# One load for the first inputs instead of two, and 13 warm-up products instead of 11, in a two-layer recurrence on one core

## What is computed

```python
# x: [32, 128 steps, 128], h0 = cond [32, 128], both layers start from it
xW = einsum('ntd,dg->ntg', x, Wx) + b
for t in range(128):
    a = xW[:, t] + h @ Wh                       # gates i, f, o, g
    c = sigmoid(f) * c + sigmoid(i) * tanh(g)   # c starts at zero
    h = sigmoid(o) * tanh(c)
x1 = x + hs
for t in range(128):
    m = concat(x1[:, t], u) @ weight + bias
    g, c = sigmoid(m[:, :128] + 1), tanh(m[:, 128:])
    u = g * u + (1 - g) * c
out = x1 + us
```

## Time and profile before

| | us |
|---|---|
| median of 3 runs (lowest to highest) | 231.49 (231.38 to 232.12) |
| the profiled execution's own time | 231.94 |
| its span, first to last instruction | 230.0 |
| PE busy | 225.1 (98%) |
| DVE busy | 200.3 (87%) |
| ACT busy | 133.8 (58%) |

### The profile page before, as it was taken

How to read it: one execution, slowest core, us unless ns; L and a number is a source line. 1 busy time by engine, 2 the same in 40 slices (tenths; PEclk the granted TensorE clock), 3 DMA queues, 4 the chain that set the end, 5 groups by cost and what they waited for, 6 DMA issues and landing times.

```text
span 230.0 us, 12260 instructions
## 1 busy us (share of the span) xinstructions
PE 225.1 (98%) x4825; PEld 212.0 (92%) x4825; DVE 200.3 (87%) x1363; ACT 133.8 (58%) x905; POOL 2.7 (1%) x11
## 2 busy tenths in 40 slices
PE   7999999999999999999999999999999999999994
PEld 6999999999999999999999999999999999999883
DVE  5457899989899999999999899999989999998995
ACT  3534665656665665666566566666656666666652
POOL 2200000000000000000000000000000000000000
PEclk9999999999999999999999999999999999999998
DMA  5100001100010000100010000100001000010001
GB/s 170 39 3 17 26 25 39 26 27 26 16 48 26 16 27 26 50 14 26 27 38 26 26 26 16 48 26 16 26 26 51 14 26 26 17 26 14 16 3 26
DMA packets 12164, 6.69 MB, mean 29 GB/s; under 512 B 1606, under 2 KB 12108, under 8 KB 12108
## 3 DMA queue, kind: packets, MB, share of 16 engines
q1 hardware_dynamic: 11952, 5.72, 8.8%
q10 hardware_dynamic: 156, 0.20, 0.2%
HBM read 3.82 MB, written 2.10 MB: 26 GB/s over the span
## 4 chain that ended last, share of the span: by engine, by line
DVE 79%; PE 9%; ACT 5%; issue 5%; DMA 1%; SPq 0%
DVE cell_bank L662 10%; DVE acts L691 10%; DVE h_low L676 10%; DVE hT L669 9%; DVE scan_add L656 7%; DVE pair L683 6%; DVE pair L685 6%; DVE h_high L670 6%; DVE u_rest L697 5%; ACT act_bank L570 5%; DVE u_low L702 3%; DVE x1T L710 3%; DVE outT L719 2%; DMA early<-in_early_dram 1%; PE a L266 1%
## 5 line engine op out<-in xcount | busy, mean ns | idle before, releaser
L282 PE MATMUL gate_f<-hT,w_f 128*128 128x32 f32 x254 | 48.8, 275 | 0.5 <-DVE hT L669 0.2
L282 PEld LDWEIGHTS gate_f<-hT,w_f 128*128 128x128 f32 x254 | 39.0, 193 | 8.5 <-DVE hT L669 8.0
L550 ACT ACTIVATE gate_f<-gate_f 128x32 f32<-128x32 f32 x127 | 23.1, 182 | 40.2 <-PE gate_f L282 40.2
L570 ACT ACTIVATE act_bank<-cell_bank 128x32 f32<-128x32 f32 x128 | 23.3, 182 | 33.4 <-DVE cell_bank L662 33.4
L662 DVE TENSOR_TENSOR_SCAN cell_bank<-act_bank,scan_add 128x64 f32<-128x64 f32 x128 | 38.2, 298 | 1.0 <-ACT act_bank L550 0.9
L576 ACT ACTIVATE acts<-a 128x64 f32<-128x64 f32 x127 | 28.3, 223 | 14.4 <-PE a L309 1.1
L300 PE MATMUL a<-h_high,w1x_scaled 128*128 128x32 f16 x254 | 35.2, 177 | 0.0
L300 PE MATMUL a<-h_high,w1x_third 128*128 128x32 f16 x254 | 35.2, 177 | 0.0
L302 PE MATMUL a<-h_low,w1x_fp 128*128 128x32 f16 x254 | 35.2, 177 | 0.0
L300 PE MATMUL a<-h_high,w1x_rest 128*128 128x32 f16 x254 | 35.1, 177 | 0.0
L669 DVE TENSOR_TENSOR hT<-out_gate,act_bank 128x32 f32<-128x32 f32 x128 | 23.9, 187 | 10.6 <-ACT act_bank L570 10.6
(11 more groups left out here) (147 smaller groups left out, 1057.3 us busy)
## 6 DMA issues: line engine op xcount, KB each, us to landing
early<-in_x_dram SPq DMA_DIRECT2D x45, 64.0 KB, 1.9
out_dram<-outT SPq DMA_DIRECT2D x31, 64.0 KB, 1.6
w_raw<-in_L_cond_weight_dram SPq DMA_DIRECT2D x2, 128.0 KB, 3.4
wh_raw<-in_L_cond_Wh_dram ACTq DMA_DIRECT2D x1, 192.0 KB, 3.0
early<-in_early_dram SPq DMA_DIRECT2D x1, 144.0 KB, 2.2
early<-in_early_dram SPq DMA_DIRECT2D x1, 128.0 KB, 2.9
w_f<-in_forget_dram SPq DMA_DIRECT2D x1, 128.0 KB, 3.4
out_dram<-outT SPq DMA_DIRECT2D x1, 48.0 KB, 1.6
```

Of the source, the lines that this page charges most:

```text
L282: nc.tensor.matmul(gate_step(GATE_F, j), w_f[:, P:2 * P], hT[:, (j - 1) % RING, :], start=False, stop=True, skip_group_check=True).then_in ...
L550: return nc.scalar.activation(out, gate_step(q, j), func)
L570: nc.scalar.activation(tanh_c[:, :], cell[:, :, 1], ACT.Tanh).then_inc(tanh_c_ready, 1)
```

## The change

Both loads from `early_in` become one, of 544 columns (272 KB), which raises `x_in[0]`. The semaphore `wx_in` and PE's wait on it are gone, so that the first projection, of gate i, waits for the whole load. The number of warm-up products ahead of that wait goes from 11 to 13. The order of PE's products, the layout of the tile and everything behind are as they were.

```diff
-WARM = 11
+WARM = 13
...
-            sp.dma_start(early[:, 2 * P:3 * P + N + HS * N], early_in[:, 2 * P:]).then_inc(x_in[0], 16)
-            sp.dma_start(early[:, 0:2 * P], early_in[:, 0:2 * P]).then_inc(wx_in, 16)
+            sp.dma_start(early[:, 0:3 * P + N + HS * N], early_in).then_inc(x_in[0], 16)
             load_x(1, 1)
...
             warm(WARM)
             pe.wait_ge(x_in[0], 16)
             project0(GATE_I, 0, 3)
-            pe.wait_ge(wx_in, 16)
             project0(GATE_O, 0, HS)
             pe.wait_ge(x_in[1], 16)
             project0(GATE_G, 0, 5)
```

More of the change, by code:

```diff
@@ L118, in two_layer_recurrence @@
         x_in = [sem(f"x_in{i}") for i in range(CHUNKS)]
-        ahead_used, wx_in = sem("ahead_used"), sem("wx_in")
+        ahead_used = sem("ahead_used")
         w_f_in, wh_in, w1x_in, w1h_in = sem("w_f_in"), sem("wh_in"), sem("w1x_in"), sem("w1h_in")
```

## The result

The changed kernel took 226.00 us (median of 4 executions: 225.66, 225.83, 226.18 and 230.91), the one before 231.48 (4 executions, 231.38 to 232.12). The ratio is 0.976, with an interval of 0.973 to 0.978. It is taken over the changed kernel's executions near 226, among them a fifth, of 226.37, that the median doesn't hold; the 230.91 is left out of it, and it is also the execution whose trace was kept. It is no stray. Both kernels turn out to have two groups of times with almost nothing between them: an early group near 226 and a late one near 231.5. Over all sets of this study the changed kernel was in the early group in 17 of 22 executions, the one before in 31 of 86 (4 more lay between, at 229.8 to 230.3).

What follows compares the result with a forecast made beforehand. PE was taken to bound 4.15 to 22.5 us, then ACT and DVE. 231.94 - 4.3 - 1.3 + 0.0 = 226.3 for the profiled execution, 225.9 for the median, given as 226.0; range 225.3 to 232.2.

Steps and rivals of the forecast that it cites:

- an early rise of the clock: PE's clock rises between 3.7 and 5 us instead of about 20.4, giving 226.0 us; chance 0.41.
- The load: The merged first load, issued at 0.73 us, lands at 3.7, with bounds of 3.29 and 4.13.
- Gate i's projection and the slip: Gate i's projection, now behind the whole load, delays gate o by 0.4 us; gate g's start slips 0.0, -0.25 to +0.45.
- The warm-up: Two more products before gate i move its earliest start from 3.06 to 3.49 us, hidden behind a landing at 3.7.
- The clock's price: Early rise saves 4.3 us over six steps after the first forget sum, and 1.3 before it.
- The chance: Early rise of PE's clock at the start 0.41, by a hair over no early rise at 0.40.
- The rival with no early rise: PE's clock at the start doesn't rise early, only the slip remains: 231.2 to 232.0, most likely 231.6; chance 0.40.
- They only gain slack: Loads behind on SP's queue go out 0.45 us earlier; PE never waited for them, so they only gain slack.
- The other rivals: Early rise falling again, 228.5 (0.05); rise at 20.4 coming later, 232.6 (0.10); merged load landing late, 232.3 (0.04).
- A rise that falls again: Clock rises early, falls as PE waits after 4.5 us; half the slow steps come back, 228.5; chance 0.05.
- The time by the rule: By the skill's rule, both kernels reach full speed early, leaving only the start's slip of 0.0 us, so 231.5.

## Why the prediction was right

The forecast was 226.0, by an early rise of the clock with a chance of 0.41, and the median came out so. The mechanism, an early rise after a fuller start, is what the early traces show; that the two medians fell on either side was in part luck (see the chance below). Step by step:

**The load.** 3.7 forecast for the landing, 3.57 measured.

**Gate i's projection and the slip.** Gate g's projection moved from 4.74 to 4.64; forecast was no movement, with -0.25 to +0.45 around it. Gate i starts at 3.62 and gate o at 4.16, 0.54 us behind, of which gate g shows 0.1 coming back.

**The warm-up.** It cost nothing, as the load lands behind it or with it: the columns stop at 3.54, and gate i's projection starts at 3.54 to 3.68 in the traces of the changed kernel. PE has no pause there.

**The clock's price.** The six steps measured 14.23 us in the late trace (8.20 to 22.43) and 10.66 in the early one (6.51 to 17.17), so 3.6 and not 4.3: the first two steps take 1.9 us each at the high clock, not 1.675. The part ahead of the first forget sum gave 1.7, where I took 1.3 of 1.0 to 1.8, and its bound was not the one I named: I went by layer 1's state weights landing at 5.9, and the chain goes over `w_f`, landed at 5.53. The two errors cancel in good part: 5.3 against 5.6.

**The chance.** This was the weak place. I reasoned from a pause in one trace and took the three times shown to say nothing. The kernel before is itself early in about a third of its executions, so the change doesn't switch the rise on; it raises its share from 31 of 86 to 17 of 22, which is clear of chance. The rival with no early rise is also true, in 5 of 22 executions, at 230.9 to 231.4, just below its 231.6. The result needed at least three of four executions late before and at least three of four early after; by these shares that comes about in two sets of five. So 226.0 as a median of four was no safe forecast, and the step of 5.5 us between the medians is twice what the change gives on average.

**"They only gain slack".** This sentence on the loads behind was wrong in the early group, where `w_f` heads the chain. The early executions of the changed kernel are another 0.2% shorter than those of before (ratio 0.998, interval 0.997 to 0.999), which goes with the earlier landing of `w_f` but isn't shown to come from it alone.

**The other rivals.** No execution of the changed kernel was slower than 231.4. A rise that falls again isn't in any of the nine early traces: from 9 to 218 us no instruction of a forget sum takes more than 0.30 us, where it takes 0.40 at 1.2 GHz. The four executions of before at 229.8 to 230.3 had no trace. Their mean granted clock is on record, 0.972 in three and 0.753 in one, where its other executions on record have 0.994 or more; whether they rose in between, or rose and fell again, is open.

**The time by the rule.** With both kernels at full speed early, as the prediction reckoned by the rule on sustained matmul activity, both would take about 226 and not the 231.5 given there: the early executions of the kernel before took 226.1 to 226.9.

The Trainium skill ("TensorE: Matmul & The Clock Gate", Part 1) says that sustained matmul activity releases the throttle, and that the moment isn't tied to the kernel's start and varies from run to run. The first doesn't account for the late executions, which stay at 1.2 GHz to about 20 us with PE at 98%. The second holds, and here the two groups lie 16 us apart in the moment of the rise, which is worth 5 us, 2.2%.

What is shown and what is argued: that the two groups are the clock is shown by two traces of one program. That more warm-up products in the first 4 us make the early group frequent, with one load or two, is shown by the counts. Whether they do it by closing the pause or by streaming more columns is not, because the kernels without a pause nearly all have more columns as well. The columns are those of the warm-up products, the pause is PE's idle time behind their start, as the profile gives it:

| | columns | pause, us | early |
|---|---|---|---|
| before, two loads, 11 products | 2816 | 0.47 | 31 of 86 |
| one load, 11 | 2816 | 0.37 | 1 of 6 |
| two loads, 13 | 3328 | 0.29 | 7 of 12 |
| one load, 13 (the changed kernel) | 3328 | none | 17 of 22 |
| two loads, 11 and 3 | 3584 | none | 5 of 6 |
| one load, 14 | 3584 | none | 12 of 12 |
| two loads, 15 | 3840 | none | 12 of 12 |
| one load, 15 | 3840 | none | 12 of 12 |
| one load, 7 of f32 | 448 | none | 0 of 6 |

Only the two rows of 3328 have the same columns with and without a pause, and 7 of 12 against 17 of 22 doesn't decide it. That a PE that reads as busy isn't enough is shown by the last row; that it is for want of columns, and not for the type, is argued. The cause of the later landings with two loads is read from the windows alone.

## What to carry to other kernels

Before costing a change by the path, see whether the times of one kernel fall in two groups, and take as many executions as it needs: with three or four, one draws a group and calls it a result. In a chain of small dependent products at the start of a kernel, run warm-up products right up to the first real ones, even at the price of starting a tenth of a microsecond later, and take products that stream many columns, as those of 256 did here and the f32 ones of 32 did not. Judge such a warm-up by the share of executions that rise early, not by the best of them.

## What I had not expected of the hardware

The same program with the same first 3.5 us ran at either speed from 3.9 us on, and the slower one lasted for 16 us. A load issued 0.88 us earlier landed no earlier (5.7 and 5.5 us); but with the first one split in two there was a trough of 142 GB/s, where it was 357 with one load, and the weights behind it, issued at 2.60, landed at 6.0 in that trace, where one load and the same issue gave 5.52.
